# Fused attention and expert layer on one core: order of the projections in the loop, and the loads at the start

## The reference

```python
x = x + xattn(layernorm(x), ctx, pos, pos, Wq, Wkv, Wout, bout)   # ctx: 16 x 128 x 128
x = x + ffn(layernorm(x), gate_w, w_gate_up, w_down, ws_gate_up, ws_down)

# xattn: 32 heads of 8 values
q = (x @ Wq).reshape(b, n, 32, 8);  k, v = split(ctx @ Wkv)
q = apply_axial_rope(q, pos);       k = apply_axial_rope(k, pos)
w = softmax(einsum('bqhd,bkhd->bhqk', q, k) / sqrt(8))
out = einsum('bhqk,bkhd->bqhd', w, v).reshape(b, n, 256) @ Wout + bout
```

## Time and profile before

| | us |
|---|---|
| three runs: median | 368.56 |
| lowest, highest | 367.84, 369.81 |
| profiled execution, its own time | 369.8 |
| its span, first to last instruction | 367.8 |
| busy: PE | 315.5 (86%) |
| busy: DVE | 221.8 (60%) |
| busy: POOL | 196.3 (53%) |
| busy: ACT | 188.2 (51%) |
| mean granted clock of PE | 0.956 of 2.4 GHz |

### The profile page before, as it was taken

The page is one execution under the profiler, slowest core; times in us unless marked ns, Lnnn a source line. Parts: engine busy times, 40 slices in busy tenths (PEclk is TensorE's granted clock), DMA queues, the critical chain, the costliest instruction groups (busy, mean ns, idle before and its releaser), DMA issues. The chain is left out here.

```text
span 367.8 us, 9525 instructions
## 1 busy us (share of the span) xinstructions
PE 315.5 (86%) x3094; PEld 218.1 (59%) x3094; DVE 221.8 (60%) x621; ACT 188.2 (51%) x389; POOL 196.3 (53%) x285
## 2 busy tenths in 40 slices
PE   0668999999999999999998558889999989999930
PEld 0445777777777777777676324445765764555520
DVE  4466777676777666777777445788549044454520
ACT  4153668767668767668667375271344342233310
POOL 5569876667866667866200181053788411525460
PEclk9996999999999999999999858999999999999985
DMA  6511114454454454543210033203123275953446
GB/s 169 183 37 30 31 25 116 119 149 118 136 138 115 116 148 115 146 132 87 77 46 3 0 115 111 69 0 87 46 84 105 67 219 181 295 136 44 52 50 228
DMA packets 33292, 37.93 MB, mean 103 GB/s; under 512 B 7808, under 2 KB 27568, under 8 KB 33200
## 3 DMA queue, kind: packets, MB, share of 16 engines
q1 hardware_dynamic: 22610, 22.03, 20.6%
q10 hardware_dynamic: 8030, 11.93, 11.7%
q0 software_dynamic: 2624, 3.61, 5.9%
HBM read 26.36 MB, written 8.96 MB: 96 GB/s over the span
## 5 line engine op out<-in xcount | busy, mean ns | idle before, releaser
L405 ACT ACTIVATE pw<-bank 128x512 f32<-128x512 f32 x128 | 78.0, 615 | 53.3 <-PE bank L635 45.1
L496 DVE TENSOR_REDUCE mx<-bank 128x4 f16<-128x512 f32 x128 | 86.2, 684 | 9.6 <-PE bank L611 8.2
L624 PE MATMUL bank<-qst,kz 128*128 128x128 f16 x512 | 50.3, 221 | 0.3 <-ACT pw L405 0.2
L611 PE MATMUL bank<-kz,qst 128*128 128x512 f16 x128 | 49.6, 389 | 0.9 <-DMA kz<-kT 0.9
L624 PEld LDWEIGHTS bank<-qst,kz 128*128 128x128 f16 x512 | 36.0, 98 | 14.6 <-issue 6.8
L943 POOL DMA_INDIRECT acc<-ac,dst x16 | 23.5, 1471 | 35.3 <-ACT ac L1025 23.4
L264 POOL TENSOR_TENSOR t<-qk,RC 128x512 f32<-128x512 f32 x15 | 19.1, 1272 | 40.2 <-ACT qk L416 40.2
L503 DVE COPY mxs<-bank 8x128 f16<-8x128 f16 x64 | 13.4, 210 | 36.4 <-PE bank L615 36.4
L635 PE MATMUL bank<-pw,V 128*32 128x128 f32 x1024 | 34.6, 276 | 0.0
L1245 PE MATMUL mbank<-hT,WSG 128*128 128x512 f16 (+1 forms) x144 | 32.0, 379 | 0.0
L635 PEld LDWEIGHTS bank<-pw,V 128*32 128x32 f32 x1024 | 26.0, 109 | 7.3 <-issue 5.0
(11 more groups left out here) (192 smaller groups left out, 640.2 us busy)
## 6 DMA issues: line engine op xcount, KB each, us to landing
ring_gu<-in_L_ffn_w_gate_up ACTq DMA_DIRECT2D x20, 352.0 KB
kz<-kT SPq DMA_DIRECT2D x64, 64.0 KB, 2.0
ring_dn<-in_L_ffn_w_down ACTq DMA_DIRECT2D x10, 352.0 KB
ring_gu<-in_L_ffn_w_gate_up SPq DMA_DIRECT2D x8, 352.0 KB
X<-in_x SPq DMA_DIRECT2D x4, 512.0 KB, 8.1
table<-ac SPq DMA_DIRECT2D x8, 256.0 KB, 2.2
acc<-X SPq DMA_DIRECT2D x4, 512.0 KB, 3.7
out<-acc SPq DMA_DIRECT2D x4, 512.0 KB, 5.6
```

Of the source, the lines that this page charges most:

```text
L405: act.activation(pw[g % 4][:, :], STB[g % 2][:, :], ACT.Exp, scale=SCALE).then_inc(exp_ok, 1)
L496: dve.tensor_reduce(mx[u // 2 % 2][:, u % 2:8:2], SB[u % 2][:, :].rearrange("p (j t) -> p j t", j=4), axis=AX.X, op=ALU.max, negate=True). ...
L611: pe.matmul(SB[u % 2][:, :], qst[m.par][:, u, :], kz[m.par][:, :, u, :], start=True, stop=True).then_inc(s_mm, 1)
L624: ins = pe.matmul(STB[g % 2][:, j * P:j * P + P], kz[m.par][:, j, g, :], qst[m.par][:, g, :], start=True, stop=True)
```

## The change

In the loop:
- PE: in g 0 the order becomes `weigh_values(o)`, `transpose_xc(m3)`, `project_v(m1)`. `project_out(o)` moves from g 7 to g 6, `transpose_k(m2)` from g 6 to g 7.
- ACT: in g 0 the order behind the exponential becomes OT, xcT, V.
- DVE: the copy of kT moves from g 6 to g 7, behind that group's reduction. SP: the kz transfers wait for kT alone, in every period.

At the beginning:
- X comes in parts of 1, 3, 6 and 6 batches. WKV comes in two halves: the key half ahead of WQ, the value half with BO and WO behind all of X, on `bo_in`. PE waits for `w_in` 32 (key half and WQ) behind the first transposes, and for `bo_in` 48 at the first value product.
- The inverse standard deviation is a power with exponent -0.5 on POOL (`spread`), in three calls: batch 0, batches 1 to 3, batches 4 to 15, the last at the head of POOL's period -1. The Sqrt and its table load on ACT go, and so does the reciprocal. DVE's `statistics` ends with the variance, and `factors` makes the bias behind the power.
- PE runs matmuls on the constants whose result nobody reads (`keep_warm`): 30 before its periods, 4 behind the first transposes, 18 behind `project_q` of batch 0 and 6 behind that of batch 1, each 256 float16 columns.
- POOL clears kz behind xn of batch 0, and waits for `bo_in` 48 only then.

```diff
+XPART = [0, 1, 4, 10, NB]
@@ SP
             for c in range(4):
-                sp.dma_start(X[:, 4 * c:4 * c + 4, :], xr[:, 4 * c:4 * c + 4, :]).then_inc(x_in[c], 16)
+                part = slice(XPART[c], XPART[c + 1])
+                sp.dma_start(X[:, part, :], xr[:, part, :]).then_inc(x_in[c], 16)
                 if c == 0:
                     sp.dma_start(CT[0][:, :], ctx_in[0]).then_inc(ctx_in_s[0], 16)
+                    sp.dma_start(WKV[:, 0:D], wkv[:, 0:D]).then_inc(w_in, 16)
                     sp.dma_start(WQ[:, :, :], wq.rearrange("(c p) n -> p c n", p=P)).then_inc(w_in, 16)
-                    sp.dma_start(WKV[:, :], wkv).then_inc(w_in, 16)
...
+            sp.dma_start(WKV[:, D:], wkv[:, D:]).then_inc(bo_in, 16)
+            sp.dma_start(BO[:, :], bout...).then_inc(bo_in, 16)
+            sp.dma_start(WO[:, :, :], wout...).then_inc(bo_in, 16)
...
-                        sp.wait_ge(exp_ok, QUADS * b.n)
+                        sp.wait_ge(kT_ok, m1.n + 1)
@@ POOL
-            pool.wait_ge(bo_in, 16)
+            pool.memset(power[:, :], -0.5).then_inc(consts, 1)
+            pool.wait_ge(consts, 7)
+            def spread(a, e, k):
+                pool.wait_ge(mv1_ok, k + 1)
+                pool.tensor_tensor(rs1[:, a:e, 0], nb1[:, a:e, 0], power[:, a:e], ALU.pow).then_inc(rs1_ok, 1)
+            spread(0, 1, 0)
+            pool.wait_ge(xn_ok, 1)
+            for i in range(2):
+                pool.memset(kz[i]..., 0.0).then_inc(kz_zero, 1)
+            spread(1, 4, 1)
+            pool.wait_ge(bo_in, 48)
             def period(b):
+                if isinstance(b.n, int) and b.n == -1:
+                    spread(4, NB, 2)
@@ ACT
-            std(0, 4, 0)
...
                         act.activation(pw[g % 4][:, :], STB[g % 2][:, :], ACT.Exp, scale=SCALE).then_inc(exp_ok, 1)
+                    if g == 0 and inside(o):
+                        evac_OT(o)
+                    if g == 0 and inside(m3):
+                        evac_xcT(m3)
                     if g == 0 and inside(m1):
                         at_least(act, v_mm, m1.n + 1)
-                        act.wait_ge(consts, 6)
+                        act.wait_ge(consts, 7)
                         at_least(act, pv_mm, QUADS * b.n)
                         act.copy(Vh[m1.par][:, :, :, 0:HD], M0[:, 0:D]...).then_inc(v_ok, 1)
-                    if g == 0 and inside(m3):
-                        evac_xcT(m3)
...
-                    if g == 0 and inside(o):
-                        evac_OT(o)
@@ DVE
+            def factors(a, e, k):
                 dve.wait_ge(rs1_ok, 2 * k + 1)
                 dve.scalar_tensor_tensor(out=nb1[:, a:e, 0], in0=mv1[:, a:e, 0], scalar=-1.0, in1=rs1[:, a:e, 0],
                                          op0=ALU.mult, op1=ALU.mult).then_inc(rs1_ok, 1)
+            statistics(0, 1, 0)
+            factors(0, 1, 0)
+            ...
+            statistics(1, 4, 1)
...
-                    if g == 6 and inside(m2):
+                    if g == 7 and inside(m2):
                         evac_kT(m2)
                     if g == 3 and isinstance(b.n, int) and b.n == -3:
                         dve.wait_ge(qk_mm, 1)
                         rope(dve, m3, M1)
+                        factors(1, 4, 1)
                         split(dve, m3)
                     if g == 7 and isinstance(b.n, int) and b.n == -2:
-                        statistics(4, NB, 1)
+                        statistics(4, NB, 2)
+                        factors(4, NB, 2)
@@ PE
-            pe.wait_ge(w_in, 48)
+            def keep_warm(n):
+                for i in range(n):
+                    pe.matmul(OB[1][:, 0:2 * P], identh[:, :], identf[:, :].bitcast(F16), start=True, stop=True)
+            keep_warm(30)
...
-                    if g == 0 and inside(m1):
-                        project_v(m1)
-                    if g == 0 and inside(m3):
-                        transpose_xc(m3)
                     if g == 0 and inside(o):
                         for q in range(4, QUADS):
                             weigh_values(o, q)
+                    if g == 0 and inside(m3):
+                        transpose_xc(m3)
+                        if isinstance(b.n, int) and b.n == -3:
+                            keep_warm(4)
+                            pe.wait_ge(w_in, 32)
+                    if g == 0 and inside(m1):
+                        project_v(m1)
...
                         project_q(m3)
+                        if isinstance(b.n, int) and b.n < -1:
+                            keep_warm(18 if b.n == -3 else 6)
...
-                    if g == 6 and inside(m2):
+                    if g == 6 and inside(o):
+                        project_out(o)
+                    if g == 7 and inside(m2):
                         transpose_k(m2)
-                    if g == 7 and inside(o):
-                        project_out(o)
```

More of the change, by code:

```diff
@@ L209, in attention @@
         rs1 = sb("rs1", [P, NB, 1])
+        power = sb("power", [P, NB])
         nb1 = sb("nb1", [P, NB, 1])
@@ L225, in attention @@
         mx_zero = sem("mx_zero")
-        stat1, mv1_ok, std1, rs1_ok = sem("stat1"), sem("mv1_ok"), sem("std1"), sem("rs1_ok")
+        stat1, mv1_ok, rs1_ok = sem("stat1"), sem("mv1_ok"), sem("rs1_ok")
         turn_s, sin_s, rope_tab = sem("turn_s"), sem("sin_s"), sem("rope_tab")
@@ L357, in add_bias @@
                 pool.tensor_tensor(X[:, m.n, :], X[:, m.n, :], BO[:, :], ALU.add).then_inc(x_biased, 1)
-            pool.wait_ge(bo_in, 16)
+            pool.memset(power[:, :], -0.5).then_inc(consts, 1)
[6 more added lines that the diff above has]
+            for i in range(2):
+                pool.memset(kz[i][:, :, :, :].rearrange("p j q t -> p (j q t)").bitcast(F32), 0.0).then_inc(kz_zero, 1)
+            spread(1, 4, 1)
+            pool.wait_ge(bo_in, 48)
             def period(b):
+                if isinstance(b.n, int) and b.n == -1:
+                    spread(4, NB, 2)
                 if inside(b + 3):
                     add_bias(b + 3)
-                    if isinstance(b.n, int) and b.n == -3:
-                        for i in range(2):
-                            pool.memset(kz[i][:, :, :, :].rearrange("p j q t -> p (j q t)").bitcast(F32), 0.0).then_inc(kz_zero, 1)
                     if not (isinstance(b.n, int) and b.n == -3):
@@ L379, in _ @@
             act.activation(ang[:, :, :, :, :], turns[:, :, :, :, :], ACT.Sin, scale=TWO_PI).then_inc(sin_s, 1)
-            def std(a, e, k):
-                act.wait_ge(mv1_ok, 2 * k + 2)
-                act.activation(rs1[:, a:e, 0], nb1[:, a:e, 0], ACT.Sqrt).then_inc(std1, 1)
-            std(0, 4, 0)
             def norm(m):
-                act.wait_ge(rs1_ok, 2 if isinstance(m.n, int) and m.n < 4 else 4)
+                act.wait_ge(rs1_ok, 6 if not isinstance(m.n, int) or m.n > 3 else 4 if m.n else 2)
                 at_least(act, xcT_mm, m.n)
@@ L428, in period @@
                         norm(m4)
-                    if g == 4 and isinstance(b.n, int) and b.n == -1:
-                        std(4, NB, 1)
                     if g in (1, 4, 6) and not isinstance(b.n, int):
@@ L464, in statistics @@
                 for j in range(a, e):
-                    if j % 4 == 0:
-                        dve.wait_ge(x_in[j // 4], 16)
+                    if j in XPART:
+                        dve.wait_ge(x_in[XPART.index(j)], 16)
                     dve.bn_stats(st1[:, j, :], X[:, j, :]).then_inc(stat1, 1)
                 for j in range(a, e):
-                    dve.wait_ge(stat1, j + 1)
+                    dve.wait_ge(stat1, j + k + 1)
                     ins = dve.bn_aggr(mv1[:, j, :], st1[:, j, :])
-                ins.then_inc(mv1_ok, 1)
-                dve.wait_ge(mv1_ok, 2 * k + 1)
+                ins.then_inc(stat1, 1)
+                dve.wait_ge(stat1, e + k + 1)
                 dve.tensor_scalar(nb1[:, a:e, 0], mv1[:, a:e, 1], EPS, None, ALU.add).then_inc(mv1_ok, 1)
[L474 to L483, removed]
+            def factors(a, e, k):
                 dve.wait_ge(rs1_ok, 2 * k + 1)
@@ L486, in statistics @@
                                          op0=ALU.mult, op1=ALU.mult).then_inc(rs1_ok, 1)
-            statistics(0, 4, 0)
+            statistics(0, 1, 0)
+            factors(0, 1, 0)
+            dve.wait_ge(sin_s, 1)
+            sin = ang[:, 0].rearrange("p b a f -> p b (a f)")
+            cos = ang[:, 1].rearrange("p b a f -> p b (a f)")
+            for r in range(2):
+                dve.tensor_copy(RC[:, :, :, r], cos)
+                dve.tensor_scalar(RS[:, :, :, r], sin, -1.0 if r == 0 else 1.0, None, ALU.mult).then_inc(rope_tab, 1)
+            statistics(1, 4, 1)
             dve.wait_ge(mx_zero, 2)
@@ L600, in project_v @@
                 at_least(pe, kT_ok, m.n + 1)
+                if isinstance(m.n, int) and m.n == 0:
+                    pe.wait_ge(bo_in, 48)
```

4 lines of the change are left out of this document (2 added, 2 removed).

## The result

| | before | after |
|---|---|---|
| median of four runs, us | 368.76 | 380.67 |
| lowest, highest | 367.84, 369.81 | 378.92, 383.26 |
| profiled execution, its own time | 369.8 | 382.26 |
| its span | 367.8 | 380.4 |

A forecast was written before the change was run, and what follows sets the result against it. PE, busy 86%, was taken to bound the kernel. Lead-in +1.2 and +1.0, loop 12 x 0.51 = +6.1, tail 0: +8.3 on 369.8 gives 378.1, as a median 376.9 us; range 368.5 to 381.5.

The forecast's parts named there:

- The first edit: Loop, g 0: xcT waits for the value product, V is queued behind xcT, query transposes wait for V; +0.45 us a period.
- Rival B: Loop: POOL causes the query-transpose stop, V is in time, both stops go; -6.0 us, 362.4 to 364.8, chance 0.13.
- C: Rival: loop even, new wait absorbed by later stops, only the lead-in shows; 368.4 to 370.8 us, chance 0.12.
- The weight load behind L611: Loop, PE g 0: the load is not hidden, so L635 starts 0.31 instead of 0.22 after L611; 0.09 us.
- The second edit: Loop, g 6 and g 7: output projection covers the max-transpose stop but waits for attnT, one stop replacing another; +0.06 a period.
- The clock and the context in the lead-in: Lead-in: CT[1] holds batch 1's transposes near 15.81, half clock and fillers put keys at 21.3 instead of 19.97.
- The moved key transposes: Lead-in, period -1: at g 7 they no longer fill a reduction wait; +0.9, with xcT ahead of V 0.1: +1.0 us.
- The power of 12 columns: Lead-in, POOL: takes 0.3 us, bounds 0.1 to 1.3, first reduction about 29.1.
- The tail: Periods 14 and 15: early output projection saves about 0.4, then loses about 0.4; nothing in sum, -0.4 to +0.6 us.
- about 0.9 us of slack is left: Loop: kz transfers issued about 0.9 us later, readers at g 3 move back 0.45, still leaving about 0.9 us.
- SP's max-row transfer: Loop: issued behind the kz transfers at 3.7 instead of 3.1, needed past 6.5; costs nothing.

The follow-up runs named there:

- Experiment 3: Changed kernel with V copied ahead of xcT on ACT in g 0, nothing else: 376.96 us, ratio 1.020 to the kernel before.
- experiment 2: Changed kernel with the old order of the loop, so only the new start: 372.38 us, ratio 1.011 to the kernel before.
- experiment 4: Changed kernel with DVE's bias factors of batches 4 to 15 moved to the end of period -1: 378.15 us, ratio 1.026 to the kernel before.
- experiment 5: Changed kernel with the value product ahead of transpose_xc on PE and V ahead of xcT on ACT: 382.25 us, ratio 1.034 to the kernel before.
- experiment 6: Changed kernel with key transposes and kT back in g 6, output projection in g 7, kz transfers as before: 377.29 us, ratio 1.022.
- experiment 10: Changed kernel with V ahead of xcT on PE and ACT, and the expert load one group later: 378.58 us, ratio 1.022 to the kernel before.
- experiment 7: Changed kernel with the second context CT[1] issued right behind WQ, nothing else: 377.12 us, ratio 1.018 to the kernel before.
- number 8: Changed kernel with CT[1] early, factors late, projection/key-transpose swap undone, V first on PE and ACT, power of batches 1 to 3 before kz clearing: 366.90 us, ratio 0.993.

## Why the prediction was right, and which terms were off

- **The first edit, +0.45 a period: right, by its mechanism.** L599 at 3.46 after L636 (forecast 3.48), xcT 0.03 behind the end of L613 (0.05), V named as releaser, rivals B and C out. Experiment 3 takes V out of xcT's shadow and gets 0.41 back. Rival B read the name POOL in the earlier trace rows as the cause; with V first, PE's stop on V goes and the period shortens, with POOL unchanged.
- **The weight load behind L611, 0.09: the row held.** L647 starts 0.31 after L623 (116.33 to 116.64), not 0.22, in the changed kernel too. The Trainium skill ("TensorE: Matmul & The Clock Gate", section "Step-by-step: what each phase is for") says that loads are pulled ahead of matmuls in flight where they do not conflict; this trace doesn't show it here.
- **The second edit, +0.06: right.** L667 stands 0.26 for attnT, the max transpose of g 7 for nothing, and undoing it gives 0.055. With twelve periods the loop is +6.09, forecast +6.1.
- **The clock and the context in the lead-in: right.** Batch 1's transposes at 15.94, its pair 0.66, six fillers of 1.28 from start to start, statistics +1.27 (forecast +1.3). The fillers behind batch 0's projections ended at 13.14, not at 12.3, so the gap was 2.80 and not over 3. Some of this is luck. Half clock was a choice of 2 to 1, and of the seven profiled kernels with this start only this one and experiment 2 took 0.66 for the pair. Experiments 3, 4, 5, 6 and 10 took 0.41, and their granted clock over 16 to 20 us was 0.57 to 1.00.
- **The moved key transposes, +1.0: right.** From first maximum to query transposes 8.33 instead of 7.28, +1.05, and experiment 6, with the transposes back in g 6, takes 7.29. How it splits into 0.9 and the 0.1 of xcT ahead of V isn't shown: with V first and the transposes left in g 7 (experiment 3) it is 7.51.
- **The power of 12 columns, 0.3: the failed term of the sum.** It took 2.28, beyond the bound of 1.3. The nearest rows I had were additions and copies, another operation. POOL was free at 28.36 (28.3 was right), so the first maximum came at 31.28 instead of 29.1: +2.2 of the 4.2 by which the profiled execution missed (382.26 against 378.1); the tail's 0.9 and the mixture's 1.1 are the others.
- **The tail, 0: low by 0.9.** The step that failed is "about 0.9 us of slack is left" for kz. It holds in full periods. In periods 13 and 14, where PE's period shrinks to 10.8, L623 stood 0.46 at 190.62, the moment at which the last kz transfer landed, and experiment 6, without the edit, shows no such stop and 0.45 less over the two periods. The other half lies behind them (+0.32): there L667 stands 0.50 for attnT ahead of the last exponential.
- **SP's max-row transfer, nothing: right for this change only.** The stop at L599 covered it. Once experiment 5 removed that stop, the transfer beside the expert load cost all that V had won.
- **The mixture, +1.1, was in no term**, and its code isn't touched. From the last output projection to the end it takes 160.2 in before, 159.6 in experiment 7, 160.0 in 6 and 163.7 in 3: it follows no edit here, and I leave it open.

## What to carry to other kernels

When a step is moved on one engine, write out the order of its copies on the engine behind it and look for semaphores that were always met in the old order: here the copy for batch b+3 began to wait for the product of batch b+1, and everything queued behind that copy waited too. An earlier start is worth only what the next gate lets through, so move the gate first: one 64 KB transfer issued earlier brought the first maximum forward by 3.68, and with the slow power off the path it came 4.15 sooner still. Price an unfamiliar operation by its own kind or give it a wide bound, and check a slack in the periods where the cover is thinnest.

## What the runs showed of the hardware

- POOL's power on 128 partitions took 0.59, 0.87 and 2.28 us for 1, 3 and 12 columns, some 0.15 a column, where POOL's addition of 256 columns takes 0.7.
- Some DVE operations that run beside POOL's clearing of memory end only when it does. In the changed kernel a 3-column operation started at 9.39 took 2.61 and ended at 12.00, the clearing ran 8.43 to 11.97. In experiment 7 the same operation ended at 11.54, the clearing at 11.53. In number 8 a cast took 1.43 instead of 0.29 and ended at 14.70, the clearing at 14.54. Others aren't touched: the first operation of batch 0's rotation took 0.69 under the clearing (number 8, from 11.20). Beside POOL's other work in number 8 two more operations took 0.75 where they took 0.43 and 0.22 alone.
- The granted clock after an idle stretch does not follow from the gap alone. Ahead of batch 1's transposes PE stood 2.16, 2.44, 2.60, 2.67, 2.80, 3.49 and 3.60 us in experiments 5, 4, 6 and 3, the changed kernel, and experiments 10 and 2. The granted clock in 16 to 20 us was 0.57, 0.66, 1.00, 0.57, 0.50, 0.71 and 0.50. This, with the moment at which these transposes can start (14.9 to 16.3), goes with a first maximum anywhere between 28.92 and 31.62, in the changed kernel and experiments 2, 3, 5, 6 and 10, which share this start and the power's place.
- A transfer of 2 KB issued within 0.1 us of a 352 KB load came late enough to stop PE in nine periods of ten, for 0.9 on the mean; with the load issued a group later it did not.
